# Splitting the experts' weights beside the experts instead of beside the layers

## The chip, the cores and the metric

The kernel runs on one core of one Trainium2 chip. The metric is the device time of one execution in microseconds (us); lower is better. The engines are TensorE (PE; its weight loads are PEld), VectorE (DVE), ScalarE (ACT), GpSimd (POOL) and SyncE (SP, which here only issues DMAs).

## The reference

A decoder of two layers over x of shape (8, 256, 256), each sublayer followed by a residual and a layernorm. The last sublayer is a mixture of experts:

```python
x = _layernorm(x + _L0_attn_ref(x, ...))            # Nystrom attention, 6 pseudo-inverse steps
x = _layernorm(x + _L0_xattn_ref(x, ctx, ctx, ...)) # dilated attention
x = _layernorm(x + _L0_ffn_ref(x, ...))             # ternary feed-forward
x = _layernorm(x + _L1_attn_ref(x, ...))            # memory attention
x = _layernorm(x + _L1_xattn_ref(x, ctx, ctx, ...)) # gated cross attention
x = _layernorm(x + _L1_ffn_ref(x, ...))             # 8 experts, top 2
# _L1_ffn_ref:  D = 256, H = 1024, E = 8
logits = X @ Wg + bg
topv, topi = top_k(logits, 2); w = softmax(topv)
for e in range(8):
    h = silu((X * w) @ W1[e]) * ((X * w) @ W3[e])
    out += where(topi == e, h @ W2[e], 0)
```

## The kernel before

**Two stages.** The first stage, `layers_kernel`, computes everything up to the router for 8 batch elements, in two streams: stream 0 takes elements 0, 2, 4, 6 and stream 1 takes 1, 3, 5, 7, each with its own arena in SBUF and its own four PSUM banks. The second stage, `experts_kernel`, runs the experts over 23 tiles (`TILES`) of 256 token slots (`SLOTS`), and then the last layernorm.

**What sets the order.** Each engine's program in the first stage is merged from several generators: the two streams (numbers 0 and 1), the experts' weights (2), set-up and clearing (3) and the router (4). A generator yields before each step. `ORDERS` holds, for each engine, a table such as `0x4 1x2`: four steps of stream 0, two of stream 1. No engine may leave this order, so an instruction that waits holds back all that stands behind it on its engine.

**Split weights.** The experts' matmuls are done in bf16 with both operands split in two parts, high and low (high is the bf16 rounding, low is the rest rounded to bf16), and three products for each pair (`TERMS`). The weights are split in the first stage, as 96 pieces of 128x512. SP loads a piece to `e_room` (L1759), ACT casts it to the high part (L1944, `act_weights`), POOL subtracts for the low part (L1950, `pool_weights`), and SP stores both parts to the HBM tensors `parts` (L1766). There are two buffers for the pieces, so a cast waits until the parts from two pieces ago are stored.

**Slots.** The router scatters each token's row to `slots` in HBM (POOL, L1906). These 17.7 MB must be cleared first: five DMAs of 3.5 MB from a pattern (`sp_clear`, L1778).

**One tile of the experts.** PE turns the tile's rows (`turned`, L2187); ACT and DVE split them into `e_xT` (L2233, L2270). `hidden` then has 8 steps of 12 matmuls (L2201) over four PSUM banks. For each step, ACT computes the silu (L2244), DVE multiplies by the gate (L2283, `mult` below), ACT casts the product to its high part (L2238, `high` below) and DVE subtracts (L2276, `low` below); `high` and `low` of a step stand behind the silu and `mult` of the next one. `answer` has 48 matmuls (L2213); ACT copies its result and POOL adds it to `tokens` with two indirect DMAs (L2122). PE's order is `hidden` of the next tile, `turned` of the one after that, `answer` of this one. DVE's and ACT's order is the same, and `hidden` on PE waits for `e_xT` of its tile. The three weight loads of a tile are 1 MB each and already split; two sets of buffers alternate. A loop runs over pairs of tiles.

Of the kernel before, what the change touches and what calls it, by code (L numbers as in the profile page):

```python
# [48 lines left out]
E = 8  # L49
# [100 lines left out]
def merge_order(text):  # L150
# [22 lines left out]
    "dve": """0x7 1x3 0x5 1x2 0x4 3x2 1x1 0x5 1x1 0x8 3x1 0x2 3x1 1x22 3x1 1x2 3x4 0x1 3x3 0x2 3x2 0x6 3x1 0x5 3x1 0x4 3x1 0x1 3x3
    1x1 3x1 0x3 1x2 0x1 1x4 0x1 1x1 0x2 1x1 0x1 1x18 0x34 1x1 0x4 1x1 0x2 1x4 0x1 1x5 0x1 1x4 0x1 1x19 0x1 1x4 0x1 1x3 0x5
    1x1 0x3 1x1 0x12 1x22 0x6 1x3 0x2 1x1 0x2 1x1 0x1 1x1 0x1 1x3 0x1 1x1 0x1 1x1 0x2 1x1 0x1 1x1 0x2 1x4 0x2 1x2 0x2 1x2
    0x2 1x1 0x2 1x1 0x4 1x2 0x1 1x1 0x2 1x1 0x6 1x2 0x5 1x2 0x2 1x3 0x3 1x4 0x5 1x1 0x5 1x21 0x1 1x1 0x4 1x1 0x3 1x2 0x1
    1x1 4x3 0x3 4x1 0x1 4x2 1x1 0x5 1x1 0x4 1x1 0x5 1x1 0x8 4x2 0x2 1x1 4x2 1x2 4x2 1x10 0x1 1x5 0x6 1x2 0x1 1x1 0x1 1x1
    0x3 1x1 0x2 1x5 0x15 1x1 0x4 1x26 0x4 1x1 0x24 1x1 0x4 1x2 0x2 1x7 0x1 1x4 0x1 1x7 0x1 1x16 0x1 1x3 0x1 1x1 0x3 1x1
    0x7 1x1 0x10 1x21 0x6 1x3 0x2 1x1 0x2 1x1 0x1 1x1 0x1 1x3 0x1 1x1 0x1 1x1 0x2 1x1 0x1 1x1 0x1 1x1 0x1 1x3 0x1 1x2 0x2
    1x1 0x2 1x1 0x2 1x1 0x4 1x2 0x1 1x1 0x2 1x1 0x6 1x1 0x5 1x1 0x2 1x2 0x1 1x3 0x2 1x4 0x5 1x1 0x5 1x21 0x1 1x1 0x4 1x1  # L180
    0x3 1x2 0x1 1x1 4x3 0x3 4x2 0x1 4x1 1x1 4x1 0x5 1x1 0x4 1x1 0x5 1x1 0x8 4x3 0x2 1x1 4x2 1x2 4x2 1x10 0x1 1x5 0x6 1x2
    0x1 1x1 0x1 1x1 0x3 1x1 0x2 1x5 0x15 1x1 0x4 1x26 0x4 1x1 0x24 1x1 0x4 1x4 0x2 1x6 0x1 1x8 0x1 1x2 0x1 1x16 0x1 1x3
    0x1 1x1 0x3 1x1 0x7 1x1 0x10 1x21 0x6 1x3 0x2 1x1 0x2 1x1 0x1 1x1 0x1 1x3 0x1 1x1 0x1 1x1 0x2 1x1 0x1 1x1 0x1 1x1 0x1
    1x3 0x1 1x2 0x2 1x1 0x2 1x1 0x2 1x1 0x5 1x2 0x1 1x1 0x1 1x1 0x6 1x1 0x5 1x1 0x2 1x2 0x1 1x3 0x2 1x4 0x5 1x1 0x5 1x21
    0x1 1x1 0x4 1x1 0x3 1x2 0x1 1x1 4x3 0x3 4x2 0x1 4x2 1x1 0x5 1x1 0x4 1x1 0x5 1x1 0x8 4x3 0x2 1x1 4x2 1x2 4x2 1x10 0x1
    1x5 0x6 1x2 0x1 1x1 0x1 1x1 0x3 1x1 0x2 1x5 0x15 1x1 0x4 1x26 0x4 1x1 0x24 1x1 0x4 1x2 0x2 1x7 0x1 1x4 0x1 1x7 0x1
    1x16 0x1 1x3 0x1 1x1 0x3 1x1 0x7 1x1 0x10 1x21 0x6 1x3 0x2 1x1 0x2 1x1 0x1 1x1 0x1 1x4 0x1 1x1 0x1 1x1 0x1 1x1 0x2 1x1
    0x1 1x2 0x1 1x2 0x1 1x1 0x1 1x1 0x1 1x1 0x2 1x1 0x5 1x2 0x1 1x1 0x3 1x2 0x6 1x1 0x5 1x2 0x2 1x3 0x3 1x4 0x5 1x1 0x5
    1x21 0x1 1x1 0x4 1x1 0x3 1x2 0x1 1x1 4x3 1x1 4x2 1x1 4x1 1x1 4x1 1x1 4x7 2x1""",
# [1857 lines left out]
def experts_kernel(nc, a, shared):  # L2047
# [5 lines left out]
    with ctx:  # L2053
# [44 lines left out]
        with nc.Block() as block:  # L2098
# [45 lines left out]
            def _(sp):  # L2144
# [21 lines left out]
                for u in range(2):  # L2166
                    rows(0, u)
# [268 lines left out]
```

## Time and profile before

| | |
|---|---|
| median of 3 runs | 1763.68 us (1758.65 to 1769.99) |
| profiled execution | 1765.36 us, of it 1763.5 us from the first to the last instruction |
| first stage | 0 to about 1343 us; the four pairs of batch elements end at about 349, 678, 998 and 1327 |
| barrier, first loads of the second stage | 1343 to 1359 us |
| experts, 23 tiles | 1359 to 1743 us |
| last layernorm | 1743 to 1763.5 us |
| busy | PE 1435.4 us (81%), DVE 1056.8 (60%), ACT 647.7 (37%), POOL 409.5 (23%) |

The chain that ended last holds only the last layernorm, so it says nothing on the first stage. The two stages have different limits and are read apart: the windows view gives the busy times of each, the timeline shows single waits.

### The profile page before, as it was taken

What the parts mean: (1) busy time and instruction counts of PE and PEld (TensorE: products, weight loads), DVE (VectorE), ACT (ScalarE), POOL (GpSimd) and SP (SyncE); (2) the same over time, 40 slices, a digit from 0 to 9 for tenths busy, and PEclk for the clock granted to TensorE, in tenths of its full rate; (3) what the DMA queues carried; (4) which work ended last, traced back from release to release, by engine and by line L of the source; (5) the groups of instructions that cost most, each with busy time, mean ns of one, the idle gap of its engine ahead of it and who ended that gap; (6) DMA issues with size and microseconds to landing.
All of it is one profiled execution on the core that took longest, in us unless ns stands there. A gap on an engine that the chain in (4) does not pass through costs nothing. (4 is left out here: it accounts for less than half of the span.)

```text
span 1763.5 us, 46865 instructions
## 1 busy us (share of the span) xinstructions
PE 1435.4 (81%) x19776; PEld 1187.6 (67%) x19776; DVE 1056.8 (60%) x2444; ACT 647.7 (37%) x1410; POOL 409.5 (23%) x451
## 2 busy tenths in 40 slices
PE   5987985779898676997885699888572999999993
PEld 3885773559666445886763489667442888888882
DVE  5766677476756837576675666756843444344444
ACT  3223443433154343314534342244332444334431
POOL 0013141131313312112232311314112112221222
PEclk8798997879999887899997879999695999999997
DMA  7454021131021222110113112012004666766663
GB/s 264 180 194 158 26 72 37 58 101 41 28 63 32 60 73 67 46 51 26 38 38 107 61 62 63 2 38 84 13 13 165 242 209 224 251 223 211 236 197 107
DMA packets 87286, 183.46 MB, mean 104 GB/s; under 512 B 8642, under 2 KB 67266, under 8 KB 77250
## 3 DMA queue, kind: packets, MB, share of 16 engines
q1 hardware_dynamic: 75913, 165.20, 26.8%
q0 software_dynamic: 8160, 10.49, 3.0%
q10 hardware_dynamic: 3040, 5.25, 0.8%
q8 instruction: 135, 2.21, 0.5%
q14 instruction: 38, 0.30, 0.1%
HBM read 141.07 MB, written 58.21 MB: 113 GB/s over the span
## 5 line engine op out<-in xcount | busy, mean ns | idle before, releaser
L2201 PE MATMUL m_bank<-e_xT,e_w 128*128 128x256 bf16 x2208 | 245.6, 273 | 0.5 <-DVE e_xT L2270 0.5
L1950 POOL TENSOR_TENSOR e_room<-e_room 128x512 bf16<-128x512 f32 x96 | 112.9, 1181 | 547.3 <-ACT e_room L1944 547.2
L714 PE MATMUL bank<-arena 64*64 64x64 f32 (+2 forms) x6400 | 226.0, 230 | 12.9 <-DVE arena L904 3.7
L714 PEld LDWEIGHTS bank<-arena 64*64 64x64 f32 x6400 | 219.2, 141 | 23.4 <-issue 12.7
L2201 PEld LDWEIGHTS m_bank<-e_xT,e_w 128*128 128x128 bf16 x2208 | 216.3, 98 | 26.5 <-DVE e_xT L2270 0.9
L2283 DVE TENSOR_TENSOR e_h<-m_bank,e_silu 128x256 f32<-128x256 f32 x184 | 78.1, 424 | 202.1 <-ACT e_silu L2244 202.1
L2213 PE MATMUL m_bank<-m_xT,e_h 128*128 128x256 bf16 x1104 | 124.1, 273 | 0.0
L2213 PEld LDWEIGHTS m_bank<-m_xT,e_h 128*128 128x128 bf16 x1104 | 107.9, 98 | 12.3
L2244 ACT ACTIVATE e_silu<-m_bank 128x256 f32<-128x256 f32 x184 | 70.5, 383 | 124.3 <-PE m_bank L2201 124.3
L2122 POOL DMA_INDIRECT tokens<-e_y,e_ids x46 | 71.5, 1555 | 89.3 <-ACT e_y L2252 79.9
L977 ACT COPY arena<-bank 128x320 f32<-128x320 f32 (+1 forms) x96 | 37.5, 391 | 148.3 <-PE bank L714 147.9
L1593 DVE TENSOR_REDUCE arena<-bank 128x1 f32<-128x512 f32 x128 | 79.5, 681 | 16.8 <-PE bank L1504 16.4
L1664 ACT ACTIVATE arena<-bank 128x512 f32<-128x512 f32 x128 | 65.7, 612 | 56.1 <-PE bank L1529 56.1
L1033 POOL TENSOR_TENSOR rstd<-ve,neghalf 128x2 f32<-128x2 f32 x48 | 37.1, 772 | 182.7 <-DVE ve L1011 182.0
L603 PE MATMUL bank<-w_rest,arena 128*128 128x256 f32 x256 | 65.6, 404 | 16.1 <-DVE arena L1263 5.1
L2276 DVE TENSOR_TENSOR e_h<-e_h,e_h 128x256 bf16<-128x256 f32 x184 | 76.6, 416 | 3.2
L1606 DVE RECIPROCAL arena<-bank 128x256 f32<-128x256 f32 x16 | 28.1, 1757 | 77.9 <-PE bank L1550 77.5
L2238 ACT CAST e_h<-e_h 128x256 bf16<-128x256 f32 x184 | 73.1, 397 | 4.5 <-DVE e_h L2283 4.5
L1209 DVE TENSOR_REDUCE arena<-bank 128x2 f32<-128x512 f32 (+1 forms) x96 | 59.8, 681 | 15.7 <-PE bank L1076 15.7
L603 PEld LDWEIGHTS bank<-w_rest,arena 128*128 128x128 f32 x256 | 48.9, 199 | 27.5 <-DVE arena L1263 6.7
L1944 ACT CAST e_room<-e_room 128x512 bf16<-128x512 f32 x96 | 59.0, 627 | 18.6 <-DMA parts<-e_room 18.6
L1291 ACT ACTIVATE arena<-bank 128x512 f32<-128x512 f32 x96 | 50.1, 605 | 37.6 <-PE bank L1107 37.5
(303 smaller groups left out, 2803.2 us busy)
## 6 DMA issues: line engine op xcount, KB each, us to landing
e_w<-parts SPq DMA_DIRECT2D x46, 1024.0 KB, 6.1
e_room<-E SPq DMA_DIRECT2D x96, 256.0 KB, 3.2
parts<-e_room SPq DMA_DIRECT2D x192, 128.0 KB, 2.9
m_xT<-parts SPq DMA_DIRECT2D x23, 1024.0 KB, 7.3
slots<-C_empty SPq DMA_DIRECT2D x5, 3536.0 KB
e_x<-slots SPq DMA_DIRECT2D x24, 272.0 KB, 6.2
w_rest<-W_rest SPq DMA_DIRECT2D x1, 3592.0 KB, 16.6
xz<-xT SPq DMA_DIRECT2D x8, 256.0 KB, 2.8
```

The source lines that it names most:

```text
L603: last = pe.matmul(b[:, t * D:(t + 1) * D], x[:, c, t * P:(t + 1) * P], w[:, c, col:col + D], start=c == 0, stop=c == chunks - 1)
L714: last = pe.matmul(b[r, p * width:(p + 1) * width], lhs[r, 4 * g + p, :], rhs[r, 4 * g + p, :], start=True, stop=True)
L1593: dve.tensor_reduce(n["mx"][:, t, h:h + 1], b[:], axis=AX.X, op=ALU.max)\
L1664: act.activation(n["p"][:, c, g, 2 * i:2 * i + 2, :].rearrange("p k t -> p (k t)"), b[:], ACT.Exp)\
L1950: pool.tensor_tensor(out=e_parts[:, j % 2, LOW], in0=e_whole[:, j % 2], in1=e_parts[:, j % 2, HIGH], op=ALU.subtract).then_inc(sem("e_low" ...
L2122: pool.indirect_dma_start(out=a["x5"], out_offset=bass.IndirectOffsetOnAxis(ids[u][:, t:t + 1], 0), in_=yo[u][:, t, :], in_offset=None, co ...
L2201: last = pe.matmul(bank[b][:, col:col + SLOTS], w[:, wp, c, f * P:(f + 1) * P], xeT[u][:, xp, c, :], start=j == 0, stop=j == len(terms) - 1)
L2213: last = pe.matmul(bank[6 + u][:, t * D:(t + 1) * D], h[u][:, hp, f, t * P:(t + 1) * P], w2[u][:, wp, f, :], start=j == 0, stop=j == len(t ...
L2238: act.copy(h[u][:, HIGH, f, :], h32[b][:]).then_inc(hh[b], 1)
L2244: act.activation(silu[b][:], bank[b][:, 0:SLOTS], ACT.Silu).then_inc(sd[b], 1)
L2276: dve.tensor_tensor(h[u][:, LOW, f, :], h32[b][:], h[u][:, HIGH, f, :], ALU.subtract)\
L2283: dve.tensor_tensor(h32[b][:], bank[b][:, SLOTS:2 * SLOTS], silu[b][:], ALU.mult)\
```

## The change

The first stage splits no weights: `sp_weights`, `act_weights` and `pool_weights` and the `parts` tensors are gone. The experts' stage loads the weights as fp32, from an input laid out by partition, as six pieces of 128x1024 a tile (512 KB each) into six buffers `e_raw`, one for each piece. ACT casts each piece to its high part and DVE, instead of POOL, subtracts for the low part. Pieces 0 to 3 are of W1 and W3, pieces 4 and 5 of W2. `SPLIT_BESIDE` says in which step of `hidden` each is split, and whether it is of this tile (0) or the next (1). A raw buffer is loaded again once its low part has been made. The loop over pairs of tiles is written out for all 23 tiles; tokens that stood for first semaphore values are gone.

Clearing is done in 13 DMAs of 1.36 MB, each issued after a named step of batch element 0 on PE. The tables of `ORDERS` are new for all engines.

The diff, cut to its core (of the two `split` functions the first is ACT's, the second DVE's; the `hidden` is DVE's, and ACT's has its splits in the same places):

```diff
+        CLEARED_AFTER = ("n_k", "n_negT", "n_s3_3", "n_y", "n_qt0_0", "n_rw1_1", "n_rw3_1", "n_out", "d_v", "d_negT", "d_total",
+                         "f_out", "r_out")
+        share = ROOMS // len(CLEARED_AFTER)
         def sp_clear(sp):
             yield from sp_setup(sp)
-            share = ROOMS // 5
-            for i in range(5):
-                yield
+            for i, name in enumerate(CLEARED_AFTER):
+                yield
+                st[0]["bk"].await_done(sp, name)
...
-        def act_weights(act):
-            for j in range(len(pieces)):
-                yield
-                act.wait_ge(sem(f"e_whole{j % 2}"), 16 * (j // 2 + 1))
-                if j >= 2:
-                    yield
-                    act.wait_ge(sem(f"e_parts_stored{j % 2}"), 32 * (j // 2))
-                act.copy(e_parts[:, j % 2, HIGH], e_whole[:, j % 2]).then_inc(sem("e_high"), 1)
-
-        def pool_weights(pool):
-            for j in range(len(pieces)):
-                yield
-                pool.wait_ge(sem("e_high"), j + 1)
-                pool.tensor_tensor(out=e_parts[:, j % 2, LOW], in0=e_whole[:, j % 2], in1=e_parts[:, j % 2, HIGH],
-                                   op=ALU.subtract).then_inc(sem("e_low"), 1)
...
+        SPLIT_BESIDE = {1: (1, 0), 2: (1, 1), 3: (0, 4), 4: (1, 2), 5: (1, 3), 6: (0, 5)}
...
+                def weights(i, which):
+                    e = sp.value_load(shared["expert"][0:1, i:i + 1], min_val=0, max_val=E - 1)
+                    for q in which:
+                        if i:
+                            sp.wait_ge(split_low[q], i)
+                        name, own = (("E1", "E1", "E3", "E3", "E2", "E2")[q], q % 2)
+                        sp.dma_start(raw[q][:], a[name][bass.ds(e, 1), :, own * 1024:(own + 1) * 1024].rearrange("o p n -> (o p) n"))\
+                            .then_inc(raw_in[q], 16)
...
+                for i in range(TILES):
+                    if i + 2 < TILES:
+                        rows(i + 2)
+                    if i + 1 < TILES:
+                        weights(i + 1, (4, 5))
+                    if i + 2 < TILES:
+                        weights(i + 2, (0, 1, 2, 3))
...
+                def split(i, q):
+                    act.wait_ge(raw_in[q], 16 * (i + 1))
+                    act.copy(piece(HIGH, i, q), raw[q][:]).then_inc(split_high[q], 1)
...
+                def split(i, q):
+                    dve.wait_ge(split_high[q], i + 1)
+                    dve.tensor_tensor(piece(LOW, i, q), raw[q][:], piece(HIGH, i, q), ALU.subtract).then_inc(split_low[q], 1)
...
+                def hidden(i):
+                    wide = SIZES[i] * P
                     for f in range(FE):
                         b = f % 4
-                        dve.wait_ge(sd[b], i * 4 + 2 * u + f // 4 + 1)
-                        dve.tensor_tensor(h32[b][:], bank[b][:, SLOTS:2 * SLOTS], silu[b][:], ALU.mult)\
+                        dve.wait_ge(sd[b], turns(i, f))
+                        dve.tensor_tensor(h32[b][:, 0:wide], bank[b][:, SLOTS:SLOTS + wide], silu[b][:, 0:wide], ALU.mult)\
                             .then_inc(hr[b], 1)
                         if f:
-                            low(i, u, f - 1)
-                    low(i, u, FE - 1)
+                            low(i, f - 1)
+                        if f in SPLIT_BESIDE:
+                            ahead, q = SPLIT_BESIDE[f]
+                            if i + ahead < TILES:
+                                split(i + ahead, q)
+                    low(i, FE - 1)
```

DVE in the experts' stage, the eight steps of one tile from its second step on, before:

```order
L2283 TENSOR_TENSOR e_h_1<-m_bank,e_silu 128x256
L2276 TENSOR_TENSOR e_h<-e_h_0,e_h 128x256
L2283 TENSOR_TENSOR e_h_2<-m_bank,e_silu 128x256
L2276 TENSOR_TENSOR e_h<-e_h_1,e_h 128x256
L2283 TENSOR_TENSOR e_h_3<-m_bank,e_silu 128x256
L2276 TENSOR_TENSOR e_h<-e_h_2,e_h 128x256
```

and now, where L2238 is the old L2283, L2230 the old L2276 and L2219 the split:

```order
L2238 TENSOR_TENSOR e_h_1<-m_bank,e_silu 128x256
L2230 TENSOR_TENSOR e_h<-e_h_0,e_h 128x256
L2219 TENSOR_TENSOR e_w_1<-e_raw,e_w_1 128x1024
L2238 TENSOR_TENSOR e_h_2<-m_bank,e_silu 128x256
L2230 TENSOR_TENSOR e_h<-e_h_1,e_h 128x256
L2219 TENSOR_TENSOR e_w_1<-e_raw,e_w_1 128x1024
L2238 TENSOR_TENSOR e_h_3<-m_bank,e_silu 128x256
L2230 TENSOR_TENSOR e_h<-e_h_2,e_h 128x256
L2219 TENSOR_TENSOR e_w_0<-e_raw,e_w_0 128x1024
```

A subtraction of 1024 columns stands behind each of the steps 1 to 6, six in a tile.

POOL in the first stage, from the set-up of the second batch element of a stream on, before (L997 adds a residual, L1033 is the power in a layernorm):

```order
L997 TENSOR_TENSOR res<-x,rows 128x512 x2
L1889 COPY slot_rows<-c_fp 128x2x16 x2
L1950 TENSOR_TENSOR e_room<-e_room 128x512 x4
L1033 TENSOR_TENSOR rstd<-ve,neghalf 128x2
L1310 TENSOR_TENSOR res<-x,rows 128x512
```

and now (L987, L1849, L1023 and L1300 are the same four lines):

```order
L987 TENSOR_TENSOR res<-x,rows 128x512 x2
L1849 COPY slot_rows<-c_fp 128x2x16 x2
L1023 TENSOR_TENSOR rstd<-ve,neghalf 128x2
L1300 TENSOR_TENSOR res<-x,rows 128x512
```

The four subtractions of weights between them are gone.

SP in the experts' stage, one tile of the steady part, before:

```order
L2147 DMA e_x<-slots 128x2x272
L2153 ISA
L2153 DMA m_xT<-parts 128x4096
L2157 ISA
L2153 ISA
L2153 DMA e_w_0<-parts 128x4096 x2
```

and now, where the first two loads of `e_raw` are pieces 4 and 5 of the next tile and the last four are pieces 0 to 3 of the tile after that; an ISA row is a wait or a register instruction:

```order
L2088 DMA e_x<-slots 128x2x272
L2092 TENSOR_LOAD s_expert
L2092 ISA x2
L2097 ISA
L2097 DMA e_raw<-E 128x1024
L2097 ISA
L2097 DMA e_raw<-E 128x1024
L2092 TENSOR_LOAD s_expert
L2092 ISA x2
L2097 ISA
L2097 DMA e_raw<-E 128x1024
L2097 DMA e_raw<-E 128x1024 x3
```

The load of piece 0 now stands behind the load of piece 5, which waits for the last split of a tile, and behind a register load.

## Rows read from the trace of the kernel before

**Rows 1.** The page's first line.

```profile
span 1763.5 us, 46865 instructions
```

**Rows 2.** Windows: stretch, length, busy us of each engine, PEclk, DMA share, GB/s.

```profile
349.00:678.00 329.00, 264.55 (x4096) 212.18 (x4096) 219.08 (x491) 124.52 (x251) 85.81 (x86) 0.88 0.18 55
678.00:998.00 320.00, 260.02 (x4094) 209.47 (x4093) 214.89 (x489) 122.24 (x247) 82.84 (x84) 0.90 0.17 55
...
1359.00:1743.00 384.00, 374.25 (x3408) 335.40 (x3408) 157.86 (x392) 153.55 (x416) 78.84 (x93) 0.99 0.64 215
```

**Rows 3.** The page's costliest groups: count, busy us, mean ns, idle before.

```profile
L1950 POOL TENSOR_TENSOR e_room<-e_room 128x512 bf16<-128x512 f32 x96 | 112.9, 1181 | 547.3 <-ACT e_room L1944 547.2
...
L1944 ACT CAST e_room<-e_room 128x512 bf16<-128x512 f32 x96 | 59.0, 627 | 18.6 <-DMA parts<-e_room 18.6
```

**Rows 4.** The layernorm's last step on DVE: groups by shape.

```profile
L1015 DVE TENSOR_SCALAR x<-y,mv,rstd 128x256 f32<-128x256 f32 x64 | 31.7, 536 | 12.6 <-POOL rstd L1033 12.5
...
L1015 DVE TENSOR_SCALAR y<-y,mv,rstd 128x256 f32<-128x256 f32 x16 | 14.1, 922 | 1.2 <-POOL rstd L1033 1.2
```

**Rows 5.** The same by source line: ns min/median/max.

```profile
L1015 DVE TENSOR_SCALAR x<-y,mv,rstd x64: 397/407/1294, 121.9 to 1232.5; 128x256 f32<-128x256 f32 x64
...
L1015 DVE TENSOR_SCALAR y<-y,mv,rstd x16: 406/408/3874, 340.4 to 1329.5; 128x256 f32<-128x256 f32 x16
```

**Rows 6.** Timeline at a batch boundary: start, us, instruction.

```profile
1009.76 3.53 DVE L1015 TENSOR_SCALAR y<-y,mv,rstd 128x256 f32<-128x256 f32 x2
...
1010.77 1.25 POOL L997 TENSOR_TENSOR res<-x,rows 128x512 f32<-128x512 f32 x1
1011.99 1.14 POOL L1950 TENSOR_TENSOR e_room<-e_room 128x512 bf16<-128x512 f32 x1
```

**Rows 7.** Timeline, after a clearing DMA: a cast's wait, and PE's.

```profile
119.37 0.62 ACT L1944 CAST e_room<-e_room 128x512 bf16<-128x512 f32 x1 [7.36 <-DMA parts<-e_room]
...
120.42 3.38 PE L714 MATMUL bank<-arena 64*64 64x64 f32 x63 [3.60 <-ACT arena L977]
```

**Rows 8.** Timeline of one expert tile, start of `hidden` to the next start.

```profile
1502.39 10.64 PE L2201 MATMUL m_bank<-e_xT,e_w 128*128 128x256 bf16 x96
...
1503.90 0.38 ACT L2244 ACTIVATE e_silu<-m_bank 128x256 f32<-128x256 f32 x1 [0.72 <-PE m_bank L2201]
...
1505.21 0.38 ACT L2244 ACTIVATE e_silu<-m_bank 128x256 f32<-128x256 f32 x1 [0.93 <-PE m_bank L2201]
...
1505.49 0.40 ACT L2238 CAST e_h<-e_h 128x256 bf16<-128x256 f32 x1
1505.63 0.42 DVE L2283 TENSOR_TENSOR e_h<-m_bank,e_silu 128x256 f32<-128x256 f32 x1 [0.89 <-ACT e_silu L2244]
1505.97 0.41 DVE L2276 TENSOR_TENSOR e_h<-e_h,e_h 128x256 bf16<-128x256 f32 x1
...
1514.26 0.58 ACT L2233 CAST e_xT<-m_bank 128x512 bf16<-128x512 f32 x1
1514.87 0.69 DVE L2270 TENSOR_TENSOR e_xT<-m_bank,e_xT 128x512 bf16<-128x512 f32 x1
...
1518.55 1.69 PE L2201 MATMUL m_bank<-e_xT,e_w 128*128 128x256 bf16 x14
```

**Rows 9.** By source line: 1024 columns on DVE and on ACT.

```profile
L559 DVE SCALAR_TENSOR_TENSOR w_ff<-e_room,w_ff x2: 1215/1220/1225, 66.5 to 70.6; 128x1024 bf16<-128x1024 f32 x2
...
L1278 ACT CAST arena<-arena x8: 1042/1042/1042, 139.3 to 1134.9; 128x1024 bf16<-128x1024 f32 x8
```

**Rows 10.** Timeline of SP's issues in a tile.

```profile
1514.98 0.82 SPq L2153 DMA_DIRECT2D e_w<-parts  x2
...
1516.72 0.39 SPq L2147 DMA_DIRECT2D e_x<-slots  x1
```

**Rows 11.** The page's DMA issues: count, KB each, us to landing.

```profile
e_w<-parts SPq DMA_DIRECT2D x46, 1024.0 KB, 6.1
e_room<-E SPq DMA_DIRECT2D x96, 256.0 KB, 3.2
```

More of the change, by code:

```diff
@@ L1914, in dve_table @@
             ci = t["ci"].bitcast(I32)
-            for i in range(2):
-                dve.wait_ge(sem(f"e_parts_stored{i}"), 32 * (len(pieces) // 2))
             jids = consts["jids"]
@@ L2215, in answer @@
                     last.then_inc(yf[u], 1)
[L2217 to L2227 removed]
+                turned(0)
+                turned(1)
+                hidden(0)
@@ L2229, in _ @@
+                for i in range(TILES):
+                    if i + 1 < TILES:
+                        hidden(i + 1)
+                    if i + 2 < TILES:
+                        turned(i + 2)
+                    answer(i)
             @block.scalar
             def _(act):
-                def turned(i, u):
-                    act.wait_ge(tf[u], i + 1)
-                    act.copy(xeT[u][:, HIGH].rearrange("p c s -> p (c s)"), bank[4 + u][:]).then_inc(th[u], 1)
-                def high(i, u, f):
-                    b = f % 4
-                    act.wait_ge(hr[b], i * 4 + 2 * u + f // 4 + 2)
-                    act.copy(h[u][:, HIGH, f, :], h32[b][:]).then_inc(hh[b], 1)
@@ L2247, in hidden @@
-                    high(i, u, FE - 1)
-                def answer(i, u):
-                    act.wait_ge(yf[u], i + 2)
-                    act.wait_ge(moved[u], i + 1)
-                    act.copy(yo[u][:].rearrange("p t d -> p (t d)"), bank[6 + u][:]).then_inc(ye[u], 1)
-                for u in range(2):
-                    turned(0, u)
-                hidden(0, 0)
-                with act.Fori(0, TURNS) as i:
-                    hidden(i, 1)
-                    turned(i + 1, 0)
-                    answer(i, 0)
-                    hidden(i + 1, 0)
-                    turned(i + 1, 1)
-                    answer(i, 1)
@@ new lines, in hidden @@
+                        if f in SPLIT_BESIDE:
+                            ahead, q = SPLIT_BESIDE[f]
+                            if i + ahead < TILES:
+                                split(i + ahead, q)
+                    low(i, FE - 1)
+                for q in range(4):
+                    split(0, q)
+                turned(0)
+                turned(1)
+                hidden(0)
+                for i in range(TILES):
+                    if i + 1 < TILES:
+                        hidden(i + 1)
+                    if i + 2 < TILES:
+                        turned(i + 2)
```

431 lines of the change are left out of this document (191 added, 240 removed).

## The prediction

> **What bounds the kernel now.** I read the windows view first, since the chain that ended last covers only the final layernorm. The span is 1763.5 us [rows 1]; the profiled execution took 1765.36, and the median of the runs is 1763.68, so a change in the span is put on that median.
>
> Two stages with different limits show in the windows [rows 2]. In the experts' stage, 1359 to 1743, PE is busy 374 of 384 us at a granted clock of 0.99 (its higher level, 2.4 GHz). DVE has 158 and ACT 154 of the 384: more than half of either is free there. A tile takes 16.16 us from one start of `hidden` to the next (1518.55 - 1502.39 [rows 8]), and PE waits for nothing in it.
>
> In the first stage a pair of batch elements takes 320 to 329 us. PE is busy about 80% at a clock of 0.88 to 0.90, DVE about 67%, ACT 38%, POOL 26% [rows 2]. Nothing is full; the two streams' dependent steps on PE and DVE decide. What is removed here stands on ACT and POOL, the two engines with room.
>
> **First stage, the removed work.** 96 casts of 627 ns on ACT (59.0 us) and 96 subtractions of 1181 ns on POOL (112.9 us) go, with 288 DMA issues on SP [rows 3]. If all of it lay on the path it would give 172 us; if none, 0. Three things say how much does.
>
> (a) POOL had been idle 547 us in total just before its weight instructions, waiting for ACT [rows 3]. POOL has work queued behind them seldom. The direct queueing on POOL I put at 1 us.
>
> (b) DVE is held up by POOL. The last step of a layernorm on DVE has medians of 407 and 408 ns [rows 5] but means of 536 and 922 [rows 4]: 64 x 0.129 + 16 x 0.514 = 16.5 us lost. In one case [rows 6] the pair of DVE instructions takes 3.53 us instead of 0.8 and ends at 1013.29, just after POOL's residual add (1010.77 to 1012.02) and weight subtraction (1011.99 to 1013.13). Without the subtraction it would end 1.1 us sooner. The same happens to two-input instructions of other lines, so the loss is larger than these two groups; but part of it is caused by POOL work that stays. All such steps stand in their stream's chain. I take 15 us, between 0 (the other stream fills PE meanwhile) and 35 (twice the two groups, all on the path).
> The Trainium skill, "SBUF — State Buffer", section "Who interferes with whom", says that a DVE instruction with two SBUF inputs, or in a two-port mode, and a GpSimd instruction that reads SBUF exclude each other for a whole instruction. The trace agrees: the DVE step above ends with POOL's subtraction. By the page's rule alone every one of the 96 subtractions could hold DVE for its 1.18 us, 113 us in all, which the measured loss of 16.5 in the two groups does not bear out; the sum keeps 15.
>
> (c) ACT: a cast waited 7.36 us for the store of its parts, behind a clearing DMA, and PE 3.60 us for the ACT copy behind it [rows 7]. That is 3.6 us. The five such waits are 18.6 us together [rows 3]; the others I take as hidden. A cast of 0.6 us in front of other ACT work costs where ACT is needed at once; with ACT at 38% I take 1 us (0 to 10).
>
> **The new order** of the first stage. The places at which PE takes the streams' steps are moved mostly in the pseudo-inverse part, where PE always has matmuls of one stream or the other; the attention parts with PE's long waits for DVE keep theirs. Two pairs before differ by 9 us (320 and 329) for the same work [rows 2], so that is what small shifts are worth in a pair. I take -4, between -30 and +15.
>
> **Clearing** in 13 DMAs instead of 5 has the same bytes and no compute instruction waits for one before the first router; SP's next work behind them comes later. Nothing, apart from (c).
>
> First stage: -1 - 15 - 3.6 - 1 - 4 = -24.6.
>
> **Experts' stage, the added work.** Six pieces a tile. ACT's cast of 128x1024 is 1.04 us; DVE's subtraction has the shape of L559, 1.22 us [rows 9]. In a DVE queue that waits for nothing the next start comes 0.34 us after a start of 0.42 (1505.63 to 1505.97 [rows 8]), 0.08 before its end, so a split takes 1.14 of DVE's time and a `mult` or `low` 0.34. DVE: 16 x 0.34 + 0.61 + 6 x 1.14 = 12.9 us of 16.16. ACT: 16 x 0.3 + 1 + 6 x 0.94 = 11.4. Both fit by their sums. But `hidden` on PE waits for `e_xT` of its tile, and DVE makes that behind all eight steps. So follow a tile, from PE's start of `hidden` as 0:
>
> - The first silu starts at 1.51, the next at 2.82 (1505.21 - 1502.39), the first `high` at 3.10 [rows 8]. The cast of piece 0 starts 0.31 later, 3.41, and ends 4.45. DVE's split of it starts at 4.49.
> - From there DVE is never short of work: 6 splits, `mult` 2 to 7, `low` 1 to 6: 6 x 1.14 + 12 x 0.34 = 10.9, to 15.4. ACT's step of 1.53 stays ahead of DVE's 1.82.
> - `mult` 7 ends at 15.15, `high` 7 at 15.59; ACT's turned cast (0.58) runs to 16.08, DVE's turned subtraction (0.69) from 16.12 to 16.81 [rows 8]. PE starts at about 16.86.
>
> That is 0.70 us later than 16.16: a new wait takes the place of DVE's idle time. Some 20 tiles see it: +14. With a DVE split of 1.3 instead of 1.14 it would be +33; with ACT and DVE overlapping better than I assume, 0. PE's bank waits don't bind: step 7 needs `mult` 3, done by 7.9, and starts at 9.2.
>
> **Fill.** The first two `hidden` follow each other without an `answer`, so DVE and ACT have 10.6 us for 14. The second one must wait for its splits, the first to be due at 13.0 instead of 10.5, and then for piece 0 of the third tile, whose load is issued only after the last split of the first. I put the fill at +6 (3 to 9). The first four splits lie beside the loads and the rows' transfer: 0.
>
> **DMA.** A tile moves as many bytes as before (3 MB). Piece 0 is loaded after split 5 of the tile before: DVE ends that at 14.8; issue 0.36; the register load and waits 0.9 (between the rows: 1515.80 to 1516.72 [rows 10]); so issued at 16.1. Landing is 3.2 us for 256 KB and 6.1 for 1024 KB [rows 11], 4.2 for 512 KB in proportion: 20.3. ACT needs it at 16.86 + 3.41 = 20.3. A tie; I take 0.
>
> Experts: +14 + 6 = +20. Sum: -24.6 + 20 = -4.6, which from the median of 1763.7 is **1759 us**.
>
> **The rivals.**
>
> *The first stage gives more.* Casts and subtractions freed, the streams run as in the best pair or better: (b) at 30, order at -15, ACT 5 more, so -55.6 + 20: 1728. For it: the loss in DVE is real and each layernorm is serial. Against: PE's waits stay where they were.
>
> *The raw loads bind (slower).* If 512 KB land like the 1024 KB of rows 11, after 6.1 us, piece 0 is there at 22.2, 1.9 us late. The ACT cast that waits holds the silus behind it, so DVE and then PE, in each of 20 tiles: +38, 1797. It decides from a landing of 4.2 us on; the adds to `tokens` and the rows share the DMA engines then. Against: 0.64 of DMA is busy, with long pauses.
>
> *The relief isn't on the path.* DVE's held-up steps are covered by the other stream: (b) 0 and order 0, so -5.6 + 20: 1778.
>
> *The experts absorb the splits wholly*, and the first stage gives 24.6: 1739. For it: 12.9 of 16.2 us.
>
> **How the numbers follow.** Forecast 0.42; first stage gives more 0.20; loads bind 0.14; no relief 0.12; experts absorb 0.12. About 1% (17.6 us) is what a measurement can tell here. Faster than 1746: the second and last case and a little of the first, 0.33. Slower than 1781: the loads' case, half of no relief, some of the first, 0.24. Same: 0.43. The range is 1732 to 1792: it leaves out the ends of the two far cases. The forecast's own range is 1744 to 1778.
>
> **What would show it.** In the profile after: pairs of batch elements at 315 to 323 us; layernorm step L1015 (its new line) with means near 410 and 600 ns; experts' period 16.9 us with PE waiting once a tile for `e_xT` by DVE, about 0.7 us; DVE busy some 330 us in that stage. If ACT waits for `e_raw` by DMA instead, the loads bind. I would be wrong above all if the new order of 860 steps a stream is worth more than its 4 us either way, which no row of before can tell.

## The result: 1.2% slower

| | before | after |
|---|---|---|
| median of 4 runs each, beside each other | 1763.3 us | 1785.5 us (1779.4 to 1789.0) |
| profiled execution | 1765.36 us | 1787.55 us |
| store of the rows of element 6 issued (element 7, the last, follows 12 us later) | 1326.3 us | 1288.7 us |
| PE's last matmul of the experts ends | 1734.0 us | 1756.2 us |

The ratio is 1.0119, with a 95% interval of 1.0075 to 1.0164. Ratios given here leave out two executions of one kernel (the second run of e8) that took 2250 us at a mean granted TensorE clock of 0.63, where its other four had 0.89 to 0.90; why the clock fell is not known.

The first line of the page of the kernel after answers to [rows 1]:

```profile
span 1785.7 us, 46403 instructions
```

The two stages moved in opposite directions. Up to element 6's store the kernel is 37.6 us shorter, behind it 59.8 us longer; together +22.2, which is the difference of the spans.

The windows from the start to element 7's store, before and after, by the columns of [rows 2]:

```profile
0.00:1338.30 1338.30, 1061.16 (x16368) 852.22 (x16368) 882.93 (x1988) 494.12 (x994) 319.99 (x331) 0.88 0.21 70
```

```profile
0.00:1300.40 1300.40, 1059.29 (x16368) 850.41 (x16368) 859.29 (x1988) 445.15 (x898) 204.93 (x235) 0.88 0.09 33
```

PE is busy for the same time, so nearly all of the 37.9 us between them is time that PE no longer stands without work. The same 1988 DVE instructions take 23.6 us less.

The windows of the kernel after, by the same columns as [rows 2]: three pairs of batch elements, then the experts.

```profile
333.00:650.00 317.00, 262.90 (x4092) 211.53 (x4091) 209.59 (x486) 109.01 (x221) 52.24 (x58) 0.89 0.04 12
650.00:971.00 321.00, 265.63 (x4095) 213.50 (x4094) 210.12 (x490) 109.34 (x222) 52.09 (x58) 0.89 0.04 12
971.00:1289.00 318.00, 262.71 (x4089) 211.27 (x4087) 210.60 (x490) 109.56 (x222) 51.43 (x55) 0.89 0.03 9
1321.00:1765.00 444.00, 385.92 (x3404) 333.99 (x3404) 303.33 (x528) 279.35 (x552) 78.77 (x92) 0.97 0.62 188
```

In the pairs POOL is down from 85 to 52 us, ACT from 124 to 109, and DVE from 219 to 210, although the change takes no instruction from DVE there. In the experts' stage neither DVE nor ACT is full: 303 and 279 of 444 us. PE has 58 us without work where it had 10. So the stage did not grow because the added work was too much for an engine. The timeline shows what it waits for (a row that crosses the view's end is shown up to there). This is one tile of the kernel after, from one start of `hidden` on PE to the next (L2138 is `hidden`, L2171 ACT's cast of a raw piece, L2219 DVE's split, L2224 DVE's part of `e_xT`); it answers to [rows 8]:

```profile
1512.59 1.22 DVE L2219 TENSOR_TENSOR e_w<-e_raw,e_w 128x1024 bf16<-128x1024 f32 x1
...
1515.84 9.53 PE L2138 MATMUL m_bank<-e_xT,e_w 128*128 128x256 bf16 x84 [1.69 <-DVE e_xT L2224]
...
1521.20 1.04 ACT L2171 CAST e_w<-e_raw 128x1024 bf16<-128x1024 f32 x1 [1.85 <-DMA e_raw<-E]
1522.15 0.38 ACT L2188 ACTIVATE e_silu<-m_bank 128x256 f32<-128x256 f32 x1
1522.28 1.23 DVE L2219 TENSOR_TENSOR e_w<-e_raw,e_w 128x1024 bf16<-128x1024 f32 x1 [2.43 <-ACT e_w L2171]
...
1534.55 1.70 PE L2138 MATMUL m_bank<-e_xT,e_w 128*128 128x256 bf16 x14 [1.69 <-DVE e_xT L2224]
```

ACT stands 1.85 us before the cast of piece 0, and its releaser is the DMA of `e_raw`. The silu of the next step starts only behind that cast, DVE has nothing to split, everything behind slips, and PE waits 1.69 us for `e_xT` at the next `hidden`. This tile took 18.71 us. The periods behind the fill lie between 17.1 and 20.8 us, where before they were all 16.16. The waits view of the kernel after, 1400 to 1740 us (who waits for whom: us in total, times, longest), shows that this is no single case:

```profile
ACT e_w L2171 <- DMA e_raw<-E: 30.6, 21, 3.9
...
PE m_bank L2138 <- DVE e_xT L2224: 28.9, 19, 1.7
PE m_bank L2138 <- DVE e_h L2238: 6.5, 13, 2.1
```

The page's DMA issues of the kernel after, where [rows 11] had 6.1 us for 1024 KB and 3.2 for 256 KB:

```profile
e_raw<-E SPq DMA_DIRECT2D x138, 512.0 KB, 6.5
```

Half of the size, but no less time than 1 MB took. The landings of single loads in the tile above, read from the trace (issue, then us to landing): piece 5 at 1513.97, 4.1 us; piece 0 at 1515.06, 6.1; piece 1 at 1515.59, 6.9; piece 2 at 1516.02, 8.4; piece 3 at 1516.49, 11.3. Five loads are issued within 2.5 us. The DMA view of the kernel after, 1514 to 1528 us in 40 slices (tenths busy, all 16 engines), shows what they meet:

```profile
DMA  0033899947779679998999899999999993320000
```

The engines are idle until the burst, and mostly 7 to 9 tenths busy while it lasts. The first pieces to be needed share them with the last. Over all tiles behind the fill, read from the trace, piece 4, which is issued alone (5.4 us ahead of the burst), landed in a median of 3.5 us (3.1 to 4.6); pieces 5, 0, 1, 2 and 3, the burst in its order, in medians of 3.9, 5.6, 6.9, 8.2 and 9.8. All are of one size, so the place in the burst makes the difference. Piece 0 took 4.1 to 8.2 us, and in 16 of the 19 periods behind the fill the period is 16.76 us plus the time by which its cast started later than 3.41 us after `hidden`, to within 0.01; in the other three it is 0.5 to 0.8 longer still.

### The profile page after: what moved, and what is told of

Same layout as the page of the kernel before. It is cut to its first block and busy times, and to the rows that moved or that the text cites. A ratio compares the mean times of both kernels' runs of the same rounds, so it can differ in the third digit from the quotient of the medians.

```text
span 1785.7 us, 46403 instructions
## 1 busy us (share of the span) xinstructions
PE 1445.2 (81%) x19772; PEld 1184.4 (66%) x19772; DVE 1179.9 (66%) x2581; ACT 726.4 (41%) x1451; POOL 293.9 (16%) x340
## 5 line engine op out<-in xcount | busy, mean ns | idle before, releaser
L2138 PE MATMUL m_bank<-e_xT,e_w 128*128 128x256 bf16 x2208 | 253.9, 276 | 46.8 <-DVE e_xT L2224 31.2
L2138 PEld LDWEIGHTS m_bank<-e_xT,e_w 128*128 128x128 bf16 x2208 | 214.5, 99 | 85.8 <-DVE e_xT L2224 37.1
L704 PE MATMUL bank<-arena 64*64 64x80 f32 (+2 forms) x6400 | 225.6, 231 | 3.2 <-DVE arena L843 1.8
L2219 DVE TENSOR_TENSOR e_w<-e_raw,e_w 128x1024 bf16<-128x1024 f32 x138 | 168.2, 1219 | 70.9 <-ACT e_w L2171 70.8
L2171 ACT CAST e_w<-e_raw 128x1024 bf16<-128x1024 f32 x138 | 144.1, 1044 | 60.4 <-DMA e_raw<-E 60.2
L1023 POOL TENSOR_TENSOR rstd<-ve,neghalf 128x2 f32<-128x2 f32 x48 | 37.4, 780 | 722.0 <-DVE ve L1001 721.1
L2153 PE MATMUL m_bank<-e_w,e_h 128*128 128x256 bf16 x1104 | 124.1, 273 | 0.0
L2238 DVE TENSOR_TENSOR e_h<-m_bank,e_silu 128x256 f32<-128x256 f32 x184 | 77.0, 418 | 65.4 <-ACT e_silu L2188 65.1
L2153 PEld LDWEIGHTS m_bank<-e_w,e_h 128*128 128x128 bf16 x1104 | 108.1, 98 | 12.3
L967 ACT COPY arena<-bank 128x320 f32<-128x320 f32 (+1 forms) x96 | 37.6, 392 | 159.7 <-PE bank L704 159.4
L1583 DVE TENSOR_REDUCE arena<-bank 128x1 f32<-128x512 f32 x128 | 79.7, 682 | 14.8 <-PE bank L1494 14.4
L2230 DVE TENSOR_TENSOR e_h<-e_h,e_h 128x256 bf16<-128x256 f32 x184 | 76.5, 416 | 3.2
L1199 DVE TENSOR_REDUCE arena<-bank 128x2 f32<-128x512 f32 (+1 forms) x96 | 59.8, 681 | 16.6 <-PE bank L1066 16.6
```

The source lines that it names most:

```text
L704: last = pe.matmul(b[r, p * width:(p + 1) * width], lhs[r, 4 * g + p, :], rhs[r, 4 * g + p, :], start=True, stop=True)
L1583: dve.tensor_reduce(n["mx"][:, t, h:h + 1], b[:], axis=AX.X, op=ALU.max)\
L2138: last = pe.matmul(bank[b][:, col:col + wide], w13[u][:, wp, which, c, f * P:(f + 1) * P], xeT[u][:, xp, c, 0:wide], start=j == 0, stop=j ...
L2153: last = pe.matmul(bank[6 + u][:, t * D:(t + 1) * D], h[u][:, hp, f, t * P:(t + 1) * P], w2[u][:, wp, f, :], start=j == 0, stop=j == len(t ...
L2171: act.copy(piece(HIGH, i, q), raw[q][:]).then_inc(split_high[q], 1)
L2219: dve.tensor_tensor(piece(LOW, i, q), raw[q][:], piece(HIGH, i, q), ALU.subtract).then_inc(split_low[q], 1)
```

## The experiments

Two theories on the experts' stage. **L**: piece 0 lands late, because its load stands behind piece 5's on SP and lands among four others. **V**: DVE's chain to `e_xT` (the 0.70 us of the prediction) is longer than I worked out, or DVE and ACT slow each other. On the first stage: **P**, POOL's subtractions hold DVE; **O**, the new tables; **C**, ACT's casts and the DMAs of the parts. Runs stood beside the kernel before on their own chip, whose median was 1764.8 us for e1, e2, e3 and e5, 1778.5 for e4, e6, e7 and e8, and 1779.1 for e9 and the second runs of e8 and e6; so only ratios are compared between these groups.

### e1: load a piece as soon as it has been split

SP issued pieces 4 and 5, then 0 to 3; the splits go 0, 1, 4, 2, 3, 5, so the loads of 0 and 1 stood behind a wait for the last split. Here SP follows the splits. ACT's, DVE's and PE's programs are as after.

```diff
-                    if i + 1 < TILES:
-                        weights(i + 1, (4, 5))
-                    if i + 2 < TILES:
-                        weights(i + 2, (0, 1, 2, 3))
+                    near = expert(i + 1) if i + 1 < TILES else None
+                    far = expert(i + 2) if i + 2 < TILES else None
+                    for f in sorted(SPLIT_BESIDE):
+                        ahead, q = SPLIT_BESIDE[f]
+                        if i + ahead + 1 < TILES:
+                            load(i + ahead + 1, q, far if ahead else near)
```

> The changed kernel with one edit: SP loads each raw piece again in the order in which the pieces are split (0, 1, 4, 2, 3, 5), instead of pieces 4 and 5 first and 0 to 3 behind them. Theory L (the load of piece 0 is issued too late, behind the wait for split 5 of the tile before): the expert tile's period falls from 18.7 us to about 16.9, where DVE's chain to e_xT sets it, ACT waits for no raw piece, the time is 1785 - 20 x 1.8 = about 1748. Rival D (the DMA engines don't deliver 512 KB in time whatever the order, because adds and rows share them): the period stays over 18 us and ACT still waits 2 us a tile, the time stays over 1775. Rival V (DVE is the bound by its own work): the period falls only to 17.8 or so, with DVE idle under 1 us a tile, the time is about 1768.

Measured: 1744.2 us, ratio 0.989 (0.9844 to 0.9936). The same bytes, the same instructions on every engine but SP, and 41 us less than after. The period is 16.76 us in every tile of the steady part. A start of `hidden` in e1's timeline:

```profile
1507.80 4.43 PE L2150 MATMUL m_bank<-e_xT,e_w 128*128 128x256 bf16 x39 [0.43 <-DVE e_xT L2236]
```

and the page's DMA line:

```profile
e_raw<-E SPq DMA_DIRECT2D x138, 512.0 KB, 4.7
```

No cast waits for `e_raw` in the steady part. What is left is PE's 0.43 us for `e_xT`. L holds, and V only for the 0.60 us that the period still has over 16.16. e1 both issues piece 0 earlier and spreads the loads; it doesn't say which of the two would do alone.

### e3: e1, with the last split behind `e_xT`

```diff
-        SPLIT_BESIDE = {1: (1, 0), 2: (1, 1), 3: (0, 4), 4: (1, 2), 5: (1, 3), 6: (0, 5)}
+        SPLIT_BESIDE = {1: (1, 0), 2: (1, 1), 3: (0, 4), 4: (1, 2), 5: (1, 3)}
+        SPLIT_AFTER = (0, 5)
```

Piece 5 (of W2, needed only by `answer`) is split by ACT and DVE behind their parts of `e_xT`.

> The edit of the load order, and split 5 moved out of the hidden part: ACT and DVE do it behind e_xT, where DVE waits for the next tile's first silu anyway. Theory L with the chain of DVE as the second bound: five splits instead of six stand ahead of e_xT, the chain is 1.1 us shorter than 16.9, so PE sets the period again at 16.2 us, PE waits for nothing in a tile; the experts' stage takes about 395 us and the time is about 1735. Rival V (DVE's own work is the bound): the period is no shorter than with the load order alone. Rival D: both stay over 18 us.

Measured: 1730.6 us, ratio 0.9816 (0.9767 to 0.9865), faster than both kernels. The period is 16.16 again, and PE is busy throughout; the window 1400 to 1650, first of e1, then of e3:

```profile
1400.00:1650.00 250.00, 243.57 (x2210) 215.20 (x2208) 196.62 (x345) 180.42 (x358) 51.21 (x60) 1.00 0.77 222
```

```profile
1400.00:1650.00 250.00, 250.00 (x2292) 224.55 (x2291) 204.64 (x354) 187.11 (x371) 58.96 (x64) 1.00 0.78 229
```

DVE does more here in the same time than in e1, so it was never full. It did one split too many ahead of the one result that PE waits for.

### e4: the kernel after, with loads of half the size

The order of the loads is that of the kernel after. Each load takes only 512 of its 1024 columns, and cast and split read these twice, so the other half of the weights is left out, while every engine has as much work as after.

```diff
-                        sp.dma_start(raw[q][:], a[name][bass.ds(e, 1), :, own * 1024:(own + 1) * 1024].rearrange("o p n -> (o p) n"))\
+                        sp.dma_start(raw[q][:, 0:512], a[name][bass.ds(e, 1), :, own * 1024:own * 1024 + 512].rearrange("o p n -> (o p) n"))\
```

> The changed kernel with each raw load cut to half its columns (256 KB), and ACT and DVE reading the loaded half twice; half of the weights are left out, the output isn't the reference's. Order of loads and work of the engines stay. Theory L: piece 0 lands behind piece 5 and the queue, 6.1 us after its issue, of it 4 us are bytes of pieces 5 and 0 and of the adds; with half the bytes it lands about 2 us earlier and the period falls from 18.6 to 16.8 us, where DVE's chain sets it; time about 1747. Rival (what costs is the wait to issue and a fixed latency, not the bytes): the period stays at 18 us or more.

Measured: ratio 0.9896 (0.9837 to 0.9955), as e1's. The period is 16.76 (16.75 to 16.76), again e1's. The page's DMA line of e4:

```profile
e_raw<-E SPq DMA_DIRECT2D x138, 256.0 KB, 2.4
```

The 2.4 us are the median of the 46 landings that the trace has, all of pieces 4 and 5; for pieces 0 to 3 it has none. The cast of piece 0 shows that this one was in time:

```profile
1522.17 10.65 PE L2138 MATMUL m_bank<-e_xT,e_w 128*128 128x256 bf16 x96 [0.43 <-DVE e_xT L2225]
...
1525.58 1.05 ACT L2171 CAST e_w<-e_raw 128x1024 bf16<-128x1024 f32 x1
```

It starts 3.41 us after `hidden`, without a wait. The piece was issued at 1521.40, so it landed within 4.2 us. So the wait is one for bytes: with half of them the bad order costs nothing. Whether the piece's own bytes or those of the others count is not told apart by e4; the medians by place in the burst, above, show that the others' do. Issue behind piece 5 is not enough by itself; it needs the long landing. Both a shorter landing (e4) and e1's earlier and spread issues take the whole wait away.

### e5: all clearing DMAs at once

```diff
-            for i, name in enumerate(CLEARED_AFTER):
+            for i in range(len(CLEARED_AFTER)):
                 yield
-                st[0]["bk"].await_done(sp, name)
```

> The changed kernel without the waits between the 13 clearing DMAs: all are issued one behind the other after the set-up. Nothing in the first stage waits for them, so theory: no difference, the first element's store at 333 us within 2 us, the time within 5 us of 1785. Rival: 17.7 MB at once, some 45 us of all DMA engines, hold back instruction fetches or loads, and the first pair takes 5 to 15 us longer.

Measured: 1785.9 us, ratio 1.0135 (1.0088 to 1.0182), beside 1785.5 of after; the first element's store at 334.4 us against 332.8, element 6's at 1290.3 against 1288.7. The pacing is worth nothing that can be measured.

### e2 and e8: the old tables

e2 is the kernel after with the tables of PE, DVE, ACT and POOL from before, less their steps for weights. Nothing else differs. e8 is e3 with them.

```diff
 ORDERS = {
-    "pe": """0x4 1x2 0x1 1x2 0x2 1x1 0x3 1x1 0x1 1x1 0x8 1x3 0x8 1x1 0x3 1x8 0x6 1x15 0x1 1x3 0x5 1x3 0x7 1x1 0x44 1x1 0x2 1x7 0x7
+    "pe": """0x4 1x2 0x1 1x2 0x2 1x1 0x3 1x1 0x1 1x1 0x8 1x3 0x18 1x1 0x4 1x8 0x8 1x30 0x44 1x2 0x7 1x2 0x2 1x11 0x3 1x12 0x1 1x17
...
```

> The changed kernel with the old tables for PE, DVE, ACT and POOL in the first stage; the steps of the weights' generator are empty, SP's table is the new one. The first stage's last store of tokens stood at 1326 us before and stands at 1289 now. Theory C (the gain comes from the removed work, above all from POOL no longer holding DVE): it stands at 1289 to 1295 here, the time is 1785 to 1792. Rival O (the new tables gave a good half): it stands at 1305 or later, the time is over 1800.

> The load order and the late split 5 in the experts' stage, with the old tables in the first stage. Against the same with the new tables (1730.6 us): the run with the old tables and the slow loads was 16 us over the changed kernel by medians and 12 us in the profile's first stage. Theory: 12 us, all in the first stage, time 1742, period 16.2 us. Rival: 16 us or more, 1747 and over, then the old tables also change something behind the first stage.

Measured: e2 1801.9 us, ratio 1.0218 (1.0171 to 1.0266), so 1801.9 - 1785.5 = 16 us above after (and above e5, which has the new tables and ran beside e2). Its time is as rival O has it; element 6's store, at 1300.2 us in the profiled execution, lies between the marks of C and O. e8 has a ratio of 0.9894 (0.9846 to 0.9943) against e3's 0.9816: 0.8%, 14 us. Both pairs say the same; the intervals of the two ratios together leave some 12 us either way. The windows over the last three pairs, first of after, then of e2 (whose profiled run was the fastest of its five, 1789 us) and of e8's second run:

```profile
333.00:1289.00 956.00, 791.23 (x12272) 636.30 (x12270) 630.31 (x1464) 327.91 (x663) 155.76 (x171) 0.89 0.03 11
```

```profile
341.00:1300.00 959.00, 781.14 (x12280) 627.29 (x12279) 629.56 (x1466) 328.64 (x664) 157.21 (x171) 0.90 0.03 11
```

```profile
342.00:1322.00 980.00, 791.75 (x12279) 638.57 (x12278) 629.54 (x1467) 328.45 (x664) 157.13 (x171) 0.88 0.03 11
```

DVE, ACT and POOL do the same work in all three. PE is without work for 956 - 791 = 165 us with the new tables and 178 and 188 with the old ones, which have the same first stage and still differ by 10. One group of waits shows a part of it. The waits of PE in the same stretches, of after and of e2 (L1583 of after is L1590 of e2, L1573 is L1580):

```profile
PE bank L1494 <- DVE arena L1573: 22.1, 3, 7.4
...
PE bank L1494 <- DVE arena L1583: 6.2, 12, 0.8
```

```profile
PE bank L1501 <- DVE arena L1590: 19.3, 15, 3.5
PE bank L1501 <- DVE arena L1580: 15.8, 3, 6.0
```

In the gated attention PE waited 15 times for DVE's maximum over a row, up to 3.5 us; with the new tables 12 times, 0.8 us at most, while the one long wait of a pair grew from 5 to 7 us. Together that is 35.1 us against 28.3.

### e6 and e7: the kernel before with small subtractions, and with small casts too

```diff
+                wide = PIECE if j < 2 else 2
-                pool.tensor_tensor(out=e_parts[:, j % 2, LOW], in0=e_whole[:, j % 2], in1=e_parts[:, j % 2, HIGH],
+                pool.tensor_tensor(out=e_parts[:, j % 2, LOW, 0:wide], in0=e_whole[:, j % 2, 0:wide], in1=e_parts[:, j % 2, HIGH, 0:wide],
```

e7 cuts ACT's cast in the same way. Of the low parts (in e7 of both) only the first two pieces are made.

> The kernel before, with POOL's subtraction of a piece cut from 512 columns to 2 from the third piece on. It leaves out nearly all low parts of the experts' weights, so the output isn't the reference's; all waits, casts, DMAs and the order stay. Theory C (POOL's subtractions hold DVE): the last store of tokens moves from 1326 us to 1311 or earlier, as the prediction's 15 us say, the two groups of the layernorm's last step have means under 450 and 700 ns, the time is about 1748. Rival: DVE's delays are covered by the other stream, the store stays at 1322 to 1326, the time within 5 us of before.

> As the run with the small subtraction, and ACT's cast of a piece cut to 2 columns as well (leaves out nearly all of the experts' weights, high and low). Theory: the casts were in few places in front of needed ACT work, so 1 to 5 us more are gained over the small subtraction alone. Rival A: the casts were worth as much as the subtractions, over 10 us more. With the old tables and all the work gone the store stood at 1300 us; what is missing from here to there is the DMAs, the waits for them and the semaphore steps.

Measured: e6 0.9899 (0.9838 to 0.996), e7 0.9943 (0.9916 to 0.9971). The medians are 1759.3 and 1768.5 us, so e7, for which 1 to 5 us less than e6 was expected, came out 9 us longer, though the intervals of the ratios overlap: the casts' 40 us of ACT bring nothing that shows. Of the signs expected of e6, the layernorm's two means were 461 and 640 ns (under 450 and 700), and element 6's store stood at 1317.3 us, not at 1311. The page's busy times of DVE are 1056.8 us before and 1035.9 in e6, for the same 2444 instructions. A second run of e6, in the group of e9:

> e6 once more (the kernel before with POOL's subtractions cut to 2 columns; the low parts are not made), since its runs spread over 16 us. Theory P: a ratio of 0.990 or less. Theory Q: 0.996 or more.

Measured: 0.9931 (0.9908 to 0.9954), in between. By the two runs of e6 the subtractions are worth 12 to 18 us; e7, which leaves out the casts as well, has 10.

### e9: only POOL's subtractions put back

The converse. To e8 come 96 subtractions of 128x512 on POOL, on scratch data, each behind a cast of 2 columns on ACT, at the old places; nothing is loaded or stored for them.

```diff
+        def pool_again(pool):
+            for j in range(96):
+                yield
+                ...
+                pool.wait_ge(sem("again_high"), j + 1)
+                pool.tensor_tensor(out=again[:, 768 + 256 * (j % 4):1024 + 256 * (j % 4)].bitcast(BF16), in0=again[:, 0:512], in1=again[:, 512:768].bitcast(BF16),
+                                   op=ALU.subtract).then_inc(sem("again_low"), 1)
```

> Leaves nothing out; it adds to e8 (old tables, splits in the experts' stage) what POOL did before: 96 subtractions of 128x512 on scratch data, each behind a 2-column copy on ACT, both at the places of the old tables; no loads and no stores of weights come back. Theory P (POOL's subtractions hold DVE's steps, and that is the larger part of what the removed work gives in the first stage): slower than e8 by 12 to 20 us, and the layernorm's last step L1012 back from means of 461 and 639 ns to some 536 and 900. Theory Q (the removed work gives by its DMAs and ACT's casts, and POOL's part seen in e6 was a matter of chance in the timing): within 5 us of e8.

> e8 once more, beside e9 on one chip, as the base of that comparison: all theories expect a ratio of 0.989 to before, within 0.005.

Measured: e9 1.0023 (1.0006 to 1.0039), e8 beside it 0.9906 (0.988 to 0.9931): the subtractions cost 1.17%, some 20 us, with the 96 small casts that release them. P holds. The page's busy times of e9, and of e8's second run:

```profile
PE 1451.7 (81%) x19772; PEld 1199.7 (67%) x19772; DVE 1207.9 (68%) x2581; ACT 734.8 (41%) x1547; POOL 427.8 (24%) x437
```

```profile
PE 1436.6 (81%) x19772; PEld 1191.9 (68%) x19772; DVE 1183.8 (67%) x2581; ACT 726.3 (41%) x1451; POOL 309.4 (18%) x340
```

The layernorm's last step, groups by shape, of e9:

```profile
L1013 DVE TENSOR_SCALAR x<-y,mv,rstd 128x256 f32<-128x256 f32 x64 | 32.2, 544 | 8.4 <-POOL rstd L1031 8.3
...
L1013 DVE TENSOR_SCALAR y<-y,mv,rstd 128x256 f32<-128x256 f32 x16 | 14.1, 924 | 1.2 <-POOL rstd L1031 1.2
```

and of e8's second run:

```profile
L1012 DVE TENSOR_SCALAR x<-y,mv,rstd 128x256 f32<-128x256 f32 x64 | 26.8, 461 | 8.4 <-POOL rstd L1030 8.2
...
L1012 DVE TENSOR_SCALAR y<-y,mv,rstd 128x256 f32<-128x256 f32 x16 | 9.5, 638 | 1.2 <-POOL rstd L1030 0.7 <-issue 0.4
```

The same 2581 DVE instructions take 24.1 us longer with POOL's subtractions beside them, and the kernel some 20 us. Not all of that is waiting: of the 21.5 us between the two spans (1785.5 and 1764.0), PE's busy time holds 15.1, at a mean granted clock of 0.885 against 0.894, and its time without work 6.4. All twelve executions of e9 have lower clocks (0.884 to 0.892) than the four of e8 (0.894 to 0.902). PE's matmuls are the same in both, so in these two traces more of the cost shows as slower matmuls than as waits; no run shows how the subtractions lead to the lower clock. The means of 544 and 924 ns are those of [rows 4] (536 and 922). Of the 24.1 us these two groups hold 10; (b) had taken the loss to be larger than theirs, and it is. The Trainium skill, "SBUF — State Buffer", section "Who interferes with whom", lets each hold DVE for a whole instruction; 24.1 of POOL's 113 us is what came of it here, and I take it that mostly DVE has no such instruction at that moment.

## Why the prediction was wrong

It said 1759 and no measurable change; it is 1785.5, 1.2% slower. That lies in the range, but on the side to which I gave 0.24, and it is the rival "the raw loads bind" that happened in the experts' stage.

**The step that failed** is the landing of piece 0, under DMA: "Landing is 3.2 us for 256 KB and 6.1 for 1024 KB, 4.2 for 512 KB in proportion: 20.3. ... A tie; I take 0." The issue was right: I had 16.1 us after the start of `hidden`, which is 0.76 before the next start at 16.86; it was 1515.84 - 1515.06 = 0.78 before. The landing was not: 6.1 us in this tile, 4.1 to 8.2 over the steady ones, with a median of 5.6. The cast then started at 1521.20 - 1515.84 = 5.36 instead of 3.41, so 1.95 late, and 16.76 + 1.95 is the 18.71 of that tile. The rival had 1.9 for this, partly by luck: it let 512 KB land like 1024 KB, and the runs show otherwise, since the same load took 3.5 us when issued alone; what made it 6.1 was the burst. Two things were wrong in the step. I took the landing by size alone from [rows 11], while this load is issued 1.1 us behind piece 5 and within 1.5 us of three others; interpolating in size left out the number in flight. And a tie is no zero: a landing can only be late, so the term's bounds were 0 and +38, and its middle was not 0. I had both facts, the issue behind piece 5 and the load's due time. The term of 0 measured +43 us, as the next paragraph works out.

**The other terms of the experts' stage** came out. The DVE chain makes the period 16.86 by the prediction, and 16.76 where loads don't bind (e1, e4): +12 us for 20 tiles, not +14. The fill was put at +6: between the second and third `e_xT` lie 23.8 us before and 30.1 in e1, so +6.3; in the kernel after it is 36.8, since the late loads add to it. Those other 6.7 us, and 20 tiles at 18.57 on the mean instead of 16.76, are 43 us: the cost of the order of loads, and the difference of the spans of after and e1 (1785.7 and 1742.8). Without it the forecast of +20 was near: behind element 6's store e1 takes 454.3 us against 437.2 before, +17.1.

**The first stage** gave 37.6 us instead of 24.6, between the forecast and the 55.6 of the rival; of that rival only the term for the order (-15) came out. Its terms:
- (b), POOL holding DVE, 15 us: that the subtractions lengthen DVE's instructions and the kernel is shown (e9, e6); the size is 12 to 20 us by these, and part of e9's is PE's lower clock, a way to the cost that (b) did not have. Of my signs, the layernorm's means fell to 457 and 709 ns in the kernel after, not to 410 and 600.
- (a) POOL's queueing 1, (c) the stores' wait 3.6, ACT 1: together 5.6, and the runs leave little room for them. e7 shows nothing for ACT's casts. e9 has none of the DMAs of the parts, and with its ratio of 1.0023, of which the experts' stage explains some 4 us (behind element 6's store e3 takes 441.4 us against 437.2 before), its first stage takes as long as before's. A separate run without those DMAs was not made.
- The new order, -4: it is -14 to -16 (e2, e8), each with some 12 us either way. My reason, that the attention parts "with PE's long waits for DVE keep theirs", was wrong: one group of such waits went from 3.5 us at most to 0.8. I had compared the tables by where steps moved, and had not followed who waits at these places.
- Clearing, nothing: e5 agrees.

By e9, e2 and e8, 20 + 15 = 35 of the 37.6 us have their cause; by e6's lower values it is 27 to 33. The rest is within what the runs scatter.

So the two errors went against each other: 13 us of gain too little on one side, 40 us of loss too little (59.8 instead of 20) on the other. e1 and e3 show where the loss lies: moving six DMA issues gives 43 us of it back, and moving one split 15 more (by the spans; 2 of the 15 lie in the first stage, where e1 and e3 are the same).

**What stays open:** how the 14 to 16 us of the tables divide among the places moved; why e7 is not below e6 (its ten executions had granted clocks of 0.885 to 0.902, e6's four 0.895 to 0.900); how POOL's subtractions lower PE's granted clock in e9; why the profiled run of e2 is 10 us or more below its four others.

## What to carry to other kernels

Where a buffer is loaded again once it has been used, issue the loads in the order of use: an in-order queue that waits for the last use first turns a spread of loads into a burst, and the piece needed first then shares the DMA engines with all the others. When a due time and a landing tie in an estimate, price both sides, and take the landing from loads with as many others in flight. An engine with room can still be what others wait for, as DVE was in e1 at 196.62 of 250 us: count what stands ahead of the one result that is on the path, and put the rest behind it (e3 gained 14 us over e1 by that alone).

## What the runs showed of the hardware

- 512 KB loads issued one at a time, about every 1.8 us, landed in a median of 4.7 us (e1). In the kernel after, one issued alone took a median of 3.5, and the five of a burst within 2.5 us took medians of 3.9, 5.6, 6.9, 8.2 and 9.8, by their place in it. Loads of 256 KB, alone or first of such a burst, took 2.4 (e4).
- 96 POOL subtractions of 128x512 (1.18 us each) lengthened unchanged DVE instructions by 24.1 us in all, and the kernel by some 20 (e9 against e8). Of the 21.5 us between the profiled spans 15.1 were longer busy time of PE for the same matmuls, at a mean granted clock of 0.885 against 0.894.
- DVE's split of 128x1024 took 1.22 us, as the one row of before had it [rows 9], with ACT casting 1024 columns beside it: here these two did not slow each other.
